# Latent attention with a ring of six PSUM banks, and its values multiplied token by token with a column of ones

## The chip, the cores and the metric

The kernel runs on one NeuronCore of a Trainium2 chip. A NeuronCore has a TensorE (matrix multiply; PE in the profile, and PEld for its loads of the stationary operand), a VectorE (DVE), a ScalarE (ACT), a GpSimd (POOL) and DMA queues, which run side by side and meet through semaphores. Matmul results go into PSUM, eight banks of 128 partitions by 512 float32. The metric is the device time of one execution in microseconds, and the median of several runs is compared.

## What is computed

Four layers follow one another on 8 sequences of 256 tokens of width 128: a minGRU, six blocks of local attention with a feed-forward, a latent attention with grouped heads, and a mixture of eight experts. The change touches the third one. The printed reference leaves the body of this layer to the reader, so it is given here as the kernel computes it (16 query heads, 4 key heads, head width 8, causal, scale 8^-0.5):

```
cq  = norm(x) @ Wqa ; q = rope(cq @ Wqb)            # 16 heads of 8
ckv = norm(x) @ Wkva; k, v = ckv @ Wkvb             # 4 heads of 8 each, k with rope
S   = q k^T + causal                                # per head 256 x 256
p   = exp(S - rowmax(S))
o   = (p @ v) / sum(p)
x   = x + o @ Wout + bout
```

Four query heads share one key head. The quotient o has 16 x 8 = 128 columns for each token.

## The kernel before

The latent stage is written out in Python for steps s = 1 to 11 (`pairs`). At step s the engines work on several sequences at once: s is being normalised and projected, a = s - 1 has its attention, c = s - 2 is finished (quotient, output projection, gate moments), and s - 3 and s - 4 choose their experts. `live(k)` says whether sequence s - k exists. Each engine has its own instruction stream (`lat_pe`, `lat_act`, `lat_dve`, `lat_pool`), in a fixed order written by hand. Nothing is reordered at run time.

A sequence's attention is cut into three parts, called quads here: m = 0 (first 128 tokens, four query heads for each key head, 128 keys), m = 1 and m = 2 (last 128 tokens, two query heads each, 256 keys). A quad has four groups r = 0 to 3, one for each key head. In a quad TensorE does this, in order:

- `scores`: four matmuls into banks 4 to 7 (L1429), and four that add the causal mask (L1435). They wait until all four `exp` of the quad before are done.
- small work of other sequences: normalisation transposes, projections, the gate's logits and counts (L1350, L1356, L1357, L1343, L1493, L1505, L1522, L1528, L1535).
- `values` of the quad before: L1465, see below.
- `turns`: the four tiles of p are transposed, four 128x128 transposes for each r (L1450), into bank 2 (r = 0, 2) and bank 3 (r = 1, 3). So r = 2 waits until ScalarE has copied r = 0 out of bank 2 (L1564), and r = 3 until VectorE has copied r = 1 out of bank 3 (L1651).

VectorE takes the row maxima (L1613) and ScalarE the exponentials (L1575) between scores and turns.

`values` before: the stationary operand is 32 columns wide, `cvj`, which holds v in 8 of the 32 columns and zeros in the others, and the moving operand is 128 columns of turned p. Four r go side by side into four groups of 32 columns of the array, and the result lies turned, features by tokens, in bank 1. A second set of matmuls with `conesb` (ones in place of v) makes the sums of p, one copy for each feature. In bank 1, columns 0 to 255 hold the numerators and 256 to 511 the denominators. VectorE then takes 128x256 reciprocals (L1624) and multiplies (L1626) into `con`, which is already the stationary operand of the output projection (L1522). GpSimd spreads v into `cvj` once a sequence (L1680), from `cvn`, which ScalarE copied out of PSUM (L1591).

After the latent stage the experts' stage sorts tokens and multiplies them; its code is not touched.

Of the kernel before, what the change touches and what calls it, by code (L numbers as in the profile page):

```python
# [13 lines left out]
ALU = mybir.AluOpType  # L14
# [4 lines left out]
P = 128  # L19
# [77 lines left out]
def mixed_kernel(nc, A, out):  # L97
    with ExitStack() as ctx:  # L98
# [80 lines left out]
        cvn = sb("cvn", [P, NT, KVH, QD])  # L179
        conesb = sb("conesb", [P, GRP, 32])  # L180
# [8 lines left out]
        cvj = sq[:, :, :].rearrange("p h d -> p (h d)").rearrange("p (k r j x) -> p k r j x", k=NT, r=KVH, j=GRP)  # L189
        late = attT[:, :, :].rearrange("p c k -> p (c k)")  # L190
        con, crd = late[:, 0:SEQ], late[:, SEQ:2 * SEQ]
# [6 lines left out]
        for a, b in ((t1, t2), (None, None), (pr, ob), (pr, ob)):  # L198
# [115 lines left out]
        c_mq, c_mk, c_cq, c_ck, cv_ev, c_cv = (sig(x, credit=2) for x in ("c_mq", "c_mk", "c_cq", "c_ck", "cv_ev", "c_cv"))  # L314
# [3 lines left out]
        c_vz, c_one = sig("c_vz"), sig("c_one")  # L318
# [29 lines left out]
            "pool": (tabs, ln_ve, ln_rs, sq_half, q_add, k_add, q_norm, k_norm, c_cq, c_ck, c_cv),  # L348
# [107 lines left out]
        NG = NQ * KVH  # L456

# [888 lines left out]
        def choose_logits(pe, g):  # L1346
            pe.wait_ge(g_out.sem, g_out.after(g))
            pe.wait_ge(d_ch.sem, d_ch.after(g - 1, PLACE))
            for t in range(NT):
                mm = pe.matmul(bank[3][:, t * NE:(t + 1) * NE], xnG[:, t * P:(t + 1) * P], wg[:, :], start=True, stop=True)  # L1350
            mm.then_inc(d_lmm.sem, 1)
# [12 lines left out]
        def choose_bias(dve, g):  # L1364
            dve.wait_ge(d_lmm.sem, d_lmm.after(g))
            link(dve, dve.tensor_tensor(dlg[:, :, :], bank[3][:, 0:NT * NE].rearrange("p (t e) -> p t e", t=NT),
                                        bgb[:, :].unsqueeze(1).broadcast_to([P, NT, NE]), ALU.add), g, LOGIT)
# [48 lines left out]
        def lat_pe(pe):  # L1416
            low, high = bank[0][:, 0:SEQ], bank[0][:, SEQ:2 * SEQ]

            def scores(a, ap, m):
                t, j0, nh, nk = QUADS[m]  # L1420
                G = NG * a + KVH * m
                if m == 0:
                    pe.wait_ge(c_cq.sem, c_cq.after(a))
                    pe.wait_ge(c_ckm.sem, c_ckm.after(a, 1))
                if m == 1:
                    pe.wait_ge(c_ckm.sem, c_ckm.after(a))
                pe.wait_ge(c_exp.sem, c_exp.after(G - 1))
                for r in range(KVH):
                    pe.matmul(bank[4 + r][:, :], cq[32 * r:32 * r + 32, ap * SEQ + t * P:ap * SEQ + (t + 1) * P],  # L1429
                              ckm[32 * r:32 * r + 32, ap * GRP + j0:ap * GRP + j0 + nh, 0:nk * P], start=True, stop=False,  # L1430
                              skip_group_check=True)
                for r in range(KVH):
                    tri = causal[:, t, :].rearrange("p (h b k) -> p h b k", h=nh, b=nk)[:, :, nk - 1, :]
                    diag = bank[4 + r][:, :].rearrange("p (h b k) -> p h b k", h=nh, b=nk)[:, :, nk - 1, :]
                    pe.matmul(diag, identb[:, :], tri, start=False, stop=True, skip_group_check=True).then_inc(c_s.sem, 1)  # L1435

            def turns(a, m, g):
                for r in range(KVH):
# [8 lines left out]
                    ev, n = (c_pta, c_ptd)[r % 2], 2 * (NQ * a + m) + r // 2  # L1447
                    pe.wait_ge(ev.sem, ev.after(n - 1))
                    for q in range(4):
                        mm = pe.transpose(bank[2 + r % 2][:, q * P:(q + 1) * P], cp[:, r, q * P:(q + 1) * P], ident)  # L1450
                    mm.then_inc(c_pt.sem, 1)

            def values(a, m):
                t, j0, nh, nk = QUADS[m]
                n = NQ * a + m
                pe.wait_ge(c_pta.sem, c_pta.after(2 * n + 1))
                pe.wait_ge(c_ptd.sem, c_ptd.after(2 * n + 1))
                if m == 0:
                    pe.wait_ge(c_cv.sem, c_cv.after(a))
                    pe.wait_ge(c_nrm.sem, c_nrm.after(a - 1))  # L1460
                for x in range(4):
                    j, kb = j0 + x // nk, x % nk
                    for o, ones in ((0, False), (SEQ, True)):
                        for r in range(KVH):
                            mm = pe.matmul(bank[1][32 * r:32 * r + 32, o + t * P:o + (t + 1) * P],  # L1465
                                           conesb[:, j, :] if ones else cvj[:, kb, r, j, :], cpT[r][:, x * P:(x + 1) * P],
                                           start=(m == 0 and x == 0 and not ones), stop=(x == 3), skip_group_check=True)
# [4 lines left out]
            pe.wait_ge(c_one.sem, 2)  # L1472
            pe.wait_ge(ld_late.sem, 16 * (BLANKS + 1))
            for s, par, live in pairs():
                a, c = s - 1, s - 2
                for m in range(NQ):
                    if live(1):
                        scores(a, 1 - par, m)
                    if m == 0 and live(4):
                        n = NQ * c + 2 if live(2) else NQ * NB - 1  # L1480
                        pe.wait_ge(c_ptd.sem, c_ptd.after(2 * n + 1))
                        choose_counts(pe, s - 4)
                    if m == 1 and live(3):
                        n = NQ * a if live(1) else NQ * NB - 1
                        pe.wait_ge(c_ptd.sem, c_ptd.after(2 * n + 1))
                        choose_logits(pe, s - 3)
                    if m == 0:
# [7 lines left out]
                        if live(3):  # L1495
                            n = NQ * c + 2 if live(2) else NQ * NB - 1
                            pe.wait_ge(c_pta.sem, c_pta.after(2 * n + 1))
# [9 lines left out]
                    if m == 1:  # L1507
# [6 lines left out]
                        if live(2):  # L1514
                            pe.wait_ge(c_nrm.sem, c_nrm.after(c))
# [4 lines left out]
                            for t in range(NT):  # L1520
                                y = low[:, t * P:(t + 1) * P]
                                mm = pe.matmul(y, con[:, t * P:(t + 1) * P], wout[:, :], start=True, stop=True)  # L1522
# [23 lines left out]
        def lat_act(act):  # L1546
            act.preload_act_table(ACT.Exp)
            for s, par, live in pairs():
                a = s - 1
                for m in range(NQ):  # L1550
# [11 lines left out]
                    def keep_turned(r):  # L1562
                        act.wait_ge(c_pt.sem, c_pt.after(NG * a + KVH * m + r))
                        act.activation(cpT[r], bank[2][:, :], ACT.Copy).then_inc(c_pta.sem, 1)  # L1564

                    for r in range(KVH):
                        if live(1):
                            G = NG * a + KVH * m + r
                            if m == 0 and r == KVH - 1:
                                keep_turned(0)  # L1570
# [3 lines left out]
                            for hh in range(nh):  # L1574
                                ins = act.activation(cp[:, r, hh * n:(hh + 1) * n], bank[4 + r][:, hh * n:(hh + 1) * n],  # L1575
# [11 lines left out]
                    if live(1):  # L1587
                        if m == 0:
                            act.wait_ge(c_pv.sem, c_pv.after(a))
                            act.wait_ge(c_cv.sem, c_cv.after(a - 1))  # L1590
                            act.activation(cvn[:, :, :, :].rearrange("p t r d -> p (t r d)"),  # L1591
                                           bank[0][:, SEQ:SEQ + NT * KVH * QD], ACT.Copy).then_inc(cv_ev.sem, 1)
                        if m:
                            keep_turned(0)
                        keep_turned(2)

        def lat_dve(dve):
# [3 lines left out]
            dve.wait_ge(ld_late.sem, 16 * (BLANKS + 1))  # L1601
            dve.tensor_scalar(run, cst("region"), ident[:, 0:1], None, ALU.mult)
            for s, par, live in pairs():
                a, c = s - 1, s - 2
                for m in range(NQ):
# [3 lines left out]
                    if live(1):  # L1609
                        for r in range(KVH):  # L1610
                            G = NG * a + KVH * m + r
                            dve.wait_ge(c_s.sem, c_s.after(G))
                            dve.tensor_reduce(cnb[:, r, 0:nh], bank[4 + r][:, :].rearrange("p (h k) -> p h k", h=nh), AX.X,  # L1613
# [5 lines left out]
                    if m == 0:  # L1619
                        if live(0):  # L1620
                            ln_moments(dve, LN_C + s, tokens(s))
                        if live(2):
                            dve.wait_ge(c_o.sem, c_o.after(NQ * c + 2))
                            dve.reciprocal(crd, bank[1][:, SEQ:2 * SEQ]).then_inc(c_nrm.sem, 1)  # L1624
                            dve.wait_ge(c_nrm.sem, c_nrm.after(c, 1))
                            dve.tensor_tensor(con, bank[1][:, 0:SEQ], crd, ALU.mult).then_inc(c_nrm.sem, 1)  # L1626
# [8 lines left out]
                    if m == 1 and live(2):  # L1635
                        dve.wait_ge(c_y.sem, c_y.after(c))
                        dve.tensor_tensor(acc[:, seq_cols(c)], bank[0][:, 0:SEQ], acc[:, seq_cols(c)], ALU.add).then_inc(c_res.sem, 1)
# [10 lines left out]
                    if live(1):  # L1648
                        for r in (1, 3):
                            dve.wait_ge(c_pt.sem, c_pt.after(NG * a + KVH * m + r))  # L1650
                            dve.tensor_copy(cpT[r], bank[3][:, :]).then_inc(c_ptd.sem, 1)  # L1651
                            if m == 0 and r == 1 and live(-1):
                                add_stream(dve, s + 1)
                    elif m == 0 and live(-1):
# [6 lines left out]
        def lat_pool(pool):  # L1661
# [4 lines left out]
            pool.memset(conesb[:, :, :], 0.0).then_inc(c_one.sem, 1)  # L1666
            pool.wait_ge(c_one.sem, 1)
            for j in range(GRP):
                ins = pool.memset(conesb[:, j, j * QD:(j + 1) * QD], 1.0)
            ins.then_inc(c_one.sem, 1)  # L1670
            pool.wait_ge(add_u.sem, 1)
            pool.wait_ge(ld_late.sem, 16 * (BLANKS + 1))
            pool.memset(cvj, 0.0).then_inc(c_vz.sem, 1)
            pool.wait_ge(c_vz.sem, 1)

            def values(s):
                pool.wait_ge(cv_ev.sem, cv_ev.after(s))
                hold(pool)
                for j in range(GRP):
                    ins = pool.tensor_copy(cvj[:, :, :, j, j * QD:(j + 1) * QD], cvn[:, :, :, :])  # L1680
                ins.then_inc(c_cv.sem, 1)

            for s, par, live in pairs():
                if live(0):
                    ln_rsqrt(pool, LN_C + s)
                if live(1):
                    pool.wait_ge(ln_stats.sem, ln_stats.after(ln_seq(s - 1)))
                    x = tokens(s - 1)
                    pool.tensor_tensor(x, x, boutb[:, :].unsqueeze(1).broadcast_to([P, NT, D]), ALU.add)
                    values(s - 1)  # L1690
# [328 lines left out]
```

## Time and profile before

| | |
|---|---|
| median of 3 runs | 2133.55 us (2131.57 to 2133.88) |
| profiled execution | 2131.08 us, span of the trace 2129.2 us |
| TensorE, VectorE, ScalarE, GpSimd busy | 1999.3, 1534.3, 1692.5, 1455.5 us |
| first and last scores of the latent stage begin | 1792.7 and 1992.3 us |
| its last values end | about 2002.7 us |

The trace gives for each instruction its engine, source line, operands, start and length. Idle time of an engine is put down to the instruction that released it. PEclk is the granted clock of TensorE: 1.00 is 2.4 GHz, 0.50 is 1.2 GHz. An f32 matmul leaves two records, each with a weight load of its own; a transpose leaves one. A matmul's record is longer than the time until the next one may start, since they are pipelined, so what a block costs is read from starts.

### The profile page before, as it was taken

To read this page: it belongs to the slowest core of one execution; us is meant where nothing else is said; L and a number is where in the kernel's file an instruction comes from. 1 tells how busy PE (TensorE), PEld (TensorE's weight loads), DVE (VectorE), ACT (ScalarE), POOL (GpSimd) and SP (SyncE) were. 2 spreads that over 40 slices of the span, in tenths; PEclk is the share of its full clock that TensorE was granted. 3 is DMA by queue.
4 is the path that set the end of the run, shared out by engine and by line. 5 is a ranking of instruction groups with operands and counts; after the bars stand their busy time and mean duration, and the time that the engine had idled before them with its cause. 6 is when DMAs were issued, how large, how long until landed. Compare 5 with 4: busy or idle time off the path is not lost. (4 is left out here: it accounts for less than half of the span.)

```text
span 2129.2 us, 64823 instructions
## 1 busy us (share of the span) xinstructions
PE 1999.3 (94%) x21611; PEld 1399.3 (66%) x21611; DVE 1534.3 (72%) x3516; ACT 1692.5 (79%) x4279; POOL 1455.5 (68%) x1662
## 2 busy tenths in 40 slices
PE   6799999999999999999999999999999997988696
PEld 3466666666666666666666666666666665655486
DVE  5777777777777777777777777777777764788654
ACT  3589898989898989898989898989898985655355
POOL 4687878787878787878787878777777762244343
PEclk8899999999999999999999999999999999999888
DMA  3232223222233222323222322223544242000023
GB/s 96 49 72 55 57 71 82 64 57 54 59 84 75 56 58 53 90 63 68 52 59 69 84 62 59 52 60 83 119 98 103 51 105 84 2 12 11 15 61 107
DMA packets 191396, 138.95 MB, mean 65 GB/s; under 512 B 47758, under 2 KB 183636, under 8 KB 191172
## 3 DMA queue, kind: packets, MB, share of 16 engines
q1 hardware_dynamic: 189028, 133.09, 26.4%
q0 software_dynamic: 2272, 4.72, 0.7%
q8 instruction: 42, 0.69, 0.1%
q14 instruction: 54, 0.44, 0.1%
HBM read 28.36 MB, written 14.96 MB: 20 GB/s over the span
## 5 line engine op out<-in xcount | busy, mean ns | idle before, releaser
L975 ACT ACTIVATE pr<-bank,mx 128x64 f32<-128x64 f32 x1536 | 336.9, 348 | 0.3 <-DVE mx L1078 0.2
L1160 POOL TENSOR_TENSOR qr<-t 128x512 f32<-128x512 f32 x192 | 245.8, 1280 | 130.4 <-DVE t L1058 130.3
L1057 DVE TENSOR_TENSOR t<-bank,rot_t 128x512 f32<-128x512 f32 x384 | 262.8, 684 | 99.7 <-PE bank L813 93.5
L1148 POOL TENSOR_TENSOR qr<-qr,rn 128x512 f32<-128x512 f32 x192 | 201.0, 1047 | 173.3 <-DVE rn L1029 173.3
L1058 DVE TENSOR_TENSOR t<-bank,rot_t 128x512 f32<-128x512 f32 x384 | 261.1, 680 | 0.0
L1163 POOL TENSOR_TENSOR kr<-t 128x512 f32<-128x512 f32 x192 | 245.7, 1280 | 1.0 <-DVE t L1058 1.0
L1166 POOL TENSOR_TENSOR sqh<-sq 128x512 f32<-128x512 f32 x192 | 245.6, 1279 | 0.0
L937 ACT ACTIVATE sq<-bank 128x512 f32<-128x512 f32 x192 | 114.3, 596 | 156.1 <-DVE t L1058 151.6
L983 ACT ACTIVATE kBD<-bank 64x512 f32<-64x512 f32 x384 | 229.0, 596 | 3.1 <-PE bank L530 0.8
L813 PE MATMUL bank<-wqkv,xs 128*128 128x512 f32 x384 | 208.1, 624 | 9.3 <-issue 6.4
L864 PE MATMUL bank<-kBD,qT 128*32 128x128 f32 x6144 | 207.5, 276 | 0.4 <-ACT bank L918 0.3
L878 PE MATMUL bank<-vBD,pT 128*32 128x128 f32 x6144 | 206.4, 275 | 0.2 <-ACT pT L941 0.2
L1089 DVE TENSOR_TENSOR ob<-bank,rinv 128x512 f32<-128x512 f32 x192 | 132.1, 688 | 98.4 <-PE bank L878 98.3
L1148 POOL TENSOR_TENSOR kr<-kr,rn 128x512 f32<-128x512 f32 x192 | 201.0, 1047 | 0.0
L836 PE MATMUL bank<-wqkv,xs 128*128 128x512 f32 x384 | 200.8, 605 | 0.0
L817 PE MATMUL bank<-wqkv,xs 128*128 128x512 f32 x384 | 198.7, 599 | 0.0
L864 PEld LDWEIGHTS bank<-kBD,qT 128*32 128x32 f32 x6144 | 156.1, 109 | 61.1 <-issue 60.2
L897 PE MATMUL bank<-attT,wo 128*128 128x256 f32 x768 | 186.4, 385 | 0.0
L1099 DVE TENSOR_REDUCE ss<-sqh 128x16 f32<-128x512 f32 x192 | 130.7, 681 | 75.8 <-POOL sqh L1166 70.1
L878 PEld LDWEIGHTS bank<-vBD,pT 128*32 128x32 f32 x6144 | 159.9, 110 | 33.6 <-issue 33.1
L1078 DVE TENSOR_REDUCE mx<-bank 128x8 f32<-128x512 f32 x192 | 131.8, 687 | 65.5 <-PE bank L864 65.5
L897 PEld LDWEIGHTS bank<-attT,wo 128*128 128x128 f32 x768 | 141.5, 189 | 27.3 <-ACT vS L956 8.7
(252 smaller groups left out, 4332.6 us busy)
## 6 DMA issues: line engine op xcount, KB each, us to landing
vBD<-vS SPq DMA_DIRECT2D x1152, 64.0 KB, 2.0
vBD<-vS SPq DMA_DIRECT2D x576, 32.0 KB, 1.8
wqkv<-in_L_ffn_Wqkv_dram SPq DMA_DIRECT2D x12, 768.0 KB, 6.6
rows<-const SPq DMA_DIRECT2D x4, 2244.0 KB, 11.2
wo<-in_L_ffn_Wo_dram SPq DMA_DIRECT2D x12, 256.0 KB, 2.9
t<-rows SPq DMA_DIRECT2D x39, 66.0 KB, 1.8
vBD<-in_L_ffn_W_dram SPq DMA_DIRECT2D x1, 2048.0 KB, 8.5
vBD<-in_L_ffn_W_dram SPq DMA_DIRECT2D x8, 256.0 KB, 7.1
```

What stands on the lines that cost most here:

```text
L813: pe.matmul(bank[0][:, :], xt, wqkv[:, h * 512:(h + 1) * 512], start=True, stop=True).then_inc(q_mm.sem, 1)
L864: mm = pe.matmul(bank[5][w * WIN:(w + 1) * WIN, p * P:(p + 1) * P], qT[:, slot % 2, p, w * WIN:(w + 1) * WIN], kBD[:, h, p, :, k0:k0 + 2 * ...
L878: mm = pe.matmul(bank[7][w * WIN:(w + 1) * WIN, p * P:(p + 1) * P], pT[:, p, w * WIN:(w + 1) * WIN], vBD[:, h, t * NWT + w, :, p, :], star ...
L897: mm = pe.matmul(bank[2][:, 0:SEQ], wo[:, h * HP + c, :], attT[:, h * HP + c, :], start=(c == 0), stop=(c == HP - 1))
L975: ins = act.activation(pr[:, slot % 2, hd, :], bank[5][:, hd * 64:(hd + 1) * 64], ACT.Exp, bias=mx[:, slot % 2, hd:hd + 1])
L983: ins = act.activation(kBD[64 * e:64 * e + 64, h, :, e, WIN + t * P:WIN + (t + 1) * P], bank[4][64 * e:64 * e + 64, :].rearrange("p (a b) ...
L1057: dve.tensor_tensor(t1[:, m], src, tab[:, 0, :].unsqueeze(1).broadcast_to([P, HH, DH]), ALU.mult)
L1058: dve.tensor_tensor(t2[:, m].rearrange("p h (s d) -> p h s d", s=2), swp, tab[:, 1, :].rearrange("p (s d) -> p s d", s=2).unsqueeze(1).bro ...
L1148: pool.tensor_tensor(x, x, rn[:, slot, half * HH:(half + 1) * HH].unsqueeze(2).broadcast_to([P, HH, DH]), ALU.mult).then_inc(norm.sem, 1)
L1160: pool.tensor_tensor(qr[:, slot].rearrange("p (h d) -> p h d", d=DH), t1[:, 0], t2[:, 0], ALU.add).then_inc(q_add.sem, 1)
L1163: pool.tensor_tensor(kr[:, slot], t1[:, 1], t2[:, 1], ALU.add).then_inc(k_add.sem, 1)
L1166: pool.tensor_tensor(sqh[:, :, :], sq[:, :, 0:DH // 2], sq[:, :, DH // 2:], ALU.add).then_inc(sq_half.sem, 1)
```

## The change

- The turned p and the scores share six banks in a ring, `RING = (4, 5, 6, 7, 2, 3)`. The scores of a quad take four of them, the turned tiles r = 0, 1 the two others, and r = 2, 3 the first two score banks, whose exponentials are done. No transpose waits for a copy of its own quad any more. It waits for the copies r + 2 of the quad before, and the scores r = 2, 3 wait for the copies r - 2 of the quad before.
- The copies out of PSUM are split anew: ScalarE takes (0, 2), (0, 1, 2), (0, 2) and VectorE the rest, where each took two. ScalarE's copy r = 0 of m = 0 no longer stands between two exponentials.
- `values`: turned p is now the stationary operand, 128x128, and the moving one is v with a column of ones, 9 columns (`cvo`). The result lies tokens by (head, 9), with the sum of p in the ninth column. There are 16 matmuls for each quad where there were 32. `cvj`, `conesb` and GpSimd's spreading go; ScalarE copies v straight into `cvo`.
- The reciprocal is of 128x32 elements, and the product is tokens by features. So it has to be turned for its projection: two transposes on TensorE into bank 1 (L1560 of the changed kernel), behind the turns of m = 0, and a 128x256 copy on ScalarE at the head of m = 1 (L1588). `values(a, 0)` and the projection wait for that copy (`c_keep`).
- The gate's logits move from bank 3 to bank 5, and GpSimd's addition of the bias raises `c_bias`, for which VectorE's residual waits.

```diff
+        RING = (4, 5, 6, 7, 2, 3)
+        COPY_ACT = ((0, 2), (0, 1, 2), (0, 2))
+        COPY_DVE = tuple(tuple(r for r in range(KVH) if r not in x) for x in COPY_ACT)
+        def score_bank(m, r):
+            return bank[RING[(2 * m + r) % len(RING)]]
+        def turn_bank(m, r):
+            return bank[RING[(2 * m + KVH + r) % len(RING)]] if r < 2 else score_bank(m, r - 2)
...
                 for r in range(KVH):
-                    pe.matmul(bank[4 + r][:, :], cq[...
+                    if r >= 2 and n:
+                        wait_turned(pe, *divmod(n - 1, NQ), r - 2)
+                    pe.matmul(score_bank(m, r)[:, :], cq[...
...
-                    ev, n = (c_pta, c_ptd)[r % 2], 2 * (NQ * a + m) + r // 2
-                    pe.wait_ge(ev.sem, ev.after(n - 1))
+                    n = NQ * a + m
+                    if r < 2 and n:
+                        wait_turned(pe, *divmod(n - 1, NQ), r + 2)
...
-                    for o, ones in ((0, False), (SEQ, True)):
-                        for r in range(KVH):
-                            mm = pe.matmul(bank[1][32 * r:32 * r + 32, o + t * P:o + (t + 1) * P],
-                                           conesb[:, j, :] if ones else cvj[:, kb, r, j, :], cpT[r][:, x * P:(x + 1) * P],
+                    for r in range(KVH):
+                        mm = pe.matmul(outs[:, t, r * GRP + j, :], cpT[r][:, x * P:(x + 1) * P], cvo[:, kb, r, :],
...
+                    if m == 0 and live(2):
+                        pe.wait_ge(c_nrm.sem, c_nrm.after(c))
+                        for t in range(NT):
+                            mm = pe.transpose(bank[1][:, t * P:(t + 1) * P], con[:, t].rearrange("p h d -> p (h d)"), ident)
+                        mm.then_inc(c_turn.sem, 1)
...
+                    if m == 1 and live(2):
+                        act.wait_ge(c_turn.sem, c_turn.after(s - 2))
+                        act.activation(conT, bank[1][:, 0:SEQ], ACT.Copy).then_inc(c_keep.sem, 1)
...
+                        if live(1):
+                            keep_turned(a, 0, 1)
                         if live(2):
                             dve.wait_ge(c_o.sem, c_o.after(NQ * c + 2))
-                            dve.reciprocal(crd, bank[1][:, SEQ:2 * SEQ]).then_inc(c_nrm.sem, 1)
+                            dve.reciprocal(crd, outs[:, :, :, QD]).then_inc(c_nrm.sem, 1)
```

How the change stands in TensorE's stream, at the end of the values and the turns of m = 0 in a step with all sequences live (s = 5). Before, from the last eight of the 32 value matmuls to the next scores:

```order
L1465 MATMUL bank1<-vS,sq 32x128 x4
L1465 MATMUL bank1<-vS,conesb 32x128 x4
L1505 MATMUL bank0<-wvb,ckva 128x32 x2
L1450 MATMUL bank2<-const,qr 128x128 x4
L1450 MATMUL bank3<-const,qr 128x128 x4
L1450 MATMUL bank2<-const,qr 128x128 x4
L1450 MATMUL bank3<-const,qr 128x128 x4
L1429 MATMUL bank4<-kBD 128x512
```

The same place in the changed kernel, all 16 value matmuls in one row:

```order
L1363 MATMUL bank2<-const,t1 128x128 x2
L1487 MATMUL bank1<-sq,vS 128x9 x16
L1523 MATMUL bank0<-wvb,ckva 128x32 x2
L1473 MATMUL bank2<-const,qr 128x128 x4
L1473 MATMUL bank3<-const,qr 128x128 x4
L1473 MATMUL bank4<-const,qr 128x128 x4
L1473 MATMUL bank5<-const,qr 128x128 x4
L1560 MATMUL bank1<-const,attT 128x128 x2
L1451 MATMUL bank6<-kBD 128x512
```

The four transposed tiles now have four banks, and two transposes of the quotient stand between them and the next scores.

VectorE at the same place, from the last maximum of m = 0 on, before:

```order
L1613 TENSOR_REDUCE cnb<-bank7 128x4
L394 BN_STATS lnst<-acc 128x6 x2
L400 BN_AGGR lnmv<-lnst 128x2 x2
L1624 RECIPROCAL attT<-bank1 128x256
L1626 TENSOR_TENSOR attT<-bank1,attT 128x256
L1651 COPY vS<-bank3 128x512
L1034 TENSOR_TENSOR xT<-xT,uT 128x256
L1651 COPY vS<-bank3 128x512
```

and in the changed kernel:

```order
L1638 TENSOR_REDUCE cnb<-bank7 128x4
L395 BN_STATS lnst<-acc 128x6 x2
L401 BN_AGGR lnmv<-lnst 128x2 x2
L1625 COPY vS<-bank3 128x512
L1651 RECIPROCAL attT<-bank1 128x32
L1653 TENSOR_TENSOR attT<-bank1,attT 128x256
L1625 COPY vS<-bank5 128x512
L1054 TENSOR_TENSOR xT<-xT,uT 128x256
```

The copy of r = 1 has moved ahead of the reciprocal, which is now 32 elements wide.

## Rows read from the trace of the kernel before

**Rows 1.** Stretches: length, busy PE, PEld, DVE, ACT, POOL, PEclk, DMA share, GB/s.

```profile
1792.00:1993.00 201.00, 174.10 (x2289) 119.63 (x2288) 155.47 (x382) 116.16 (x341) 69.59 (x124) 1.00 0.03 8
```

**Rows 2.** PE by line, 1792.7 to 2003: busy, mean ns, idle before, releasers.

```profile
L1450 PE MATMUL bank<-const,qr 128*128 128x128 f32 x384 | 55.2, 279 | 26.2 <-ACT vS L1564 14.8 <-DVE vS L1651 10.8 <-ACT qr L1575 0.6
```

**Rows 3.** Timeline of PE, quad m = 0: start, length, line, idle before.

```profile
1894.56 1.14 PE L1429 MATMUL bank<-kBD 32*128 32x512 f32 x8
...
1897.44 0.42 PE L1465 MATMUL bank<-vS,sq 128*32 128x128 f32 x8
...
1897.90 0.40 PE L1465 MATMUL bank<-vS,sq 128*32 128x128 f32 x8
...
1899.32 0.63 PE L1505 MATMUL bank<-wvb,ckva 32*128 32x32 f32 x4
1899.88 1.10 PE L1450 MATMUL bank<-const,qr 128*128 128x128 f32 x8
1901.94 0.63 PE L1450 MATMUL bank<-const,qr 128*128 128x128 f32 x4 [0.96 <-ACT vS L1564]
1903.03 0.63 PE L1450 MATMUL bank<-const,qr 128*128 128x128 f32 x4 [0.47 <-DVE vS L1651]
1903.59 0.71 PE L1429 MATMUL bank<-kBD 32*128 32x512 f32 x4
```

**Rows 4.** Timeline of PE, turns of a quad m = 2 and the next scores.

```profile
1891.29 1.09 PE L1450 MATMUL bank<-const,qr 128*128 128x128 f32 x8
1892.72 0.63 PE L1450 MATMUL bank<-const,qr 128*128 128x128 f32 x4 [0.34 <-ACT vS L1564]
1894.00 0.63 PE L1450 MATMUL bank<-const,qr 128*128 128x128 f32 x4 [0.65 <-DVE vS L1651]
```

**Rows 5.** The gate's logits: loads by line (ns min/median/max), and one timeline row.

```profile
L1350 PEld LDWEIGHTS bank<-wg,uT x32: 186/192/338, 1851.5 to 2016.5; 128*128 128x128 f32 x32
2002.73 0.52 PEld L1350 LDWEIGHTS bank<-wg,uT 128*128 128x128 f32 x4 [0.20 <-issue]
```

**Rows 6.** Scores on PE by line: duration ns, first and last start.

```profile
L1429 PE MATMUL bank<-kBD x192: 587/625/692, 1792.7 to 1992.7; 32*128 32x512 f32 x192
```

**Rows 7.** Timeline of DVE in the quad of rows 3, and a small reciprocal.

```profile
1900.10 1.72 DVE L1624 RECIPROCAL attT<-bank 128x256 f32<-128x256 f32 x1
1901.86 0.42 DVE L1626 TENSOR_TENSOR attT<-bank,attT 128x256 f32<-128x256 f32 x1
1902.20 0.68 DVE L1651 COPY vS<-bank 128x512 f32<-128x512 f32 x1
1750.61 0.20 DVE L1067 RECIPROCAL rinv<-psm 128x8 f32<-128x8 f32 x1
```

**Rows 8.** Timeline of ACT in the quad of rows 3.

```profile
1901.09 0.71 ACT L1564 ACTIVATE vS<-bank 128x512 f32<-128x512 f32 x1
1901.57 1.26 ACT L1575 ACTIVATE qr<-bank,cnb 128x128 f32<-128x128 f32 x4
```

**Rows 9.** Timeline at the stage's end: the last projection on PE.

```profile
2005.21 0.71 PE L1522 MATMUL bank<-wout,attT 128*128 128x128 f32 x4 [1.86 <-DVE attT L1626]
```

**Rows 10.** Stretches as in rows 1, and PE by line for two of them.

```profile
1779.50:1789.60 10.10, 8.35 (x19) 5.04 (x18) 2.35 (x4) 3.85 (x7) 6.87 (x15) 0.50 1.14 332
1796.50:1799.90 3.40, 2.22 (x16) 1.67 (x16) 1.86 (x7) 3.40 (x15) 1.61 (x3) 1.00 0.01 2
2028.70:2032.00 3.30, 3.30 (x30) 3.08 (x29) 2.74 (x8) 2.23 (x3) 1.14 (x2) 1.00 0.12 41
2032.10:2038.80 6.70, 4.52 (x21) 3.96 (x20) 4.49 (x14) 0.57 (x3) 0.00 (x0) 0.50 0.23 51
L1714 PE MATMUL bank<-b2e,vS 8*128 8x128 f32 x32 | 4.4, 299 | 0.0
```

**Rows 11.** Timeline of PE: the same twelve matmuls at either clock.

```profile
1766.51 2.96 PE L503 MATMUL bank<-xnF,w 128*128 128x256 f32 x12
1783.93 5.46 PE L503 MATMUL bank<-xnF,w 128*128 128x256 f32 x12 [0.75 <-issue]
```

More of the change, by code:

```diff
@@ L456, in mixed_kernel, with turned, wait_turned @@
         NG = NQ * KVH
+        RING = (4, 5, 6, 7, 2, 3)
[5 more added lines that the diff above has]
+            return bank[RING[(2 * m + KVH + r) % len(RING)]] if r < 2 else score_bank(m, r - 2)
+        def turned(a, m, r):
+            x, who = (c_pta, COPY_ACT) if r in COPY_ACT[m] else (c_ptd, COPY_DVE)
+            return x, sum(map(len, who)) * a + sum(map(len, who[:m])) + who[m].index(r)
+        def wait_turned(eng, a, m, r):
+            x, n = turned(a, m, r)
+            eng.wait_ge(x.sem, x.after(n))
         LAG = 3
@@ L1349, in choose_logits @@
             for t in range(NT):
-                mm = pe.matmul(bank[3][:, t * NE:(t + 1) * NE], xnG[:, t * P:(t + 1) * P], wg[:, :], start=True, stop=True)
+                mm = pe.matmul(bank[5][:, t * NE:(t + 1) * NE], xnG[:, t * P:(t + 1) * P], wg[:, :], start=True, stop=True)
             mm.then_inc(d_lmm.sem, 1)
@@ L1495, in lat_pe @@
                         if live(3):
-                            n = NQ * c + 2 if live(2) else NQ * NB - 1
-                            pe.wait_ge(c_pta.sem, c_pta.after(2 * n + 1))
+                            wait_turned(pe, c if live(2) else NB - 1, 2, 2)
                             choose_turn(pe, s - 3, 1 - par)
@@ L1589, in lat_act @@
                             act.wait_ge(c_pv.sem, c_pv.after(a))
[L1590 to L1595, printed above, removed]
+                            act.activation(cvo[:, :, :, 0:QD], bank[0][:, SEQ:SEQ + NT * KVH * QD].rearrange("p (t r d) -> p t r d", t=NT, r=KVH),
+                                           ACT.Copy).then_inc(cv_ev.sem, 1)
+                        for r in COPY_ACT[m]:
+                            act.wait_ge(c_pt.sem, c_pt.after(NG * a + KVH * m + r))
+                            act.activation(cpT[r], turn_bank(m, r)[:, :], ACT.Copy).then_inc(c_pta.sem, 1)
         def lat_dve(dve):
@@ L1636, in lat_dve @@
                         dve.wait_ge(c_y.sem, c_y.after(c))
+                        dve.wait_ge(c_bias.sem, c_bias.after(c))
                         dve.tensor_tensor(acc[:, seq_cols(c)], bank[0][:, 0:SEQ], acc[:, seq_cols(c)], ALU.add).then_inc(c_res.sem, 1)
@@ L1648, in lat_dve @@
                     if live(1):
[L1649 to L1654, printed above, removed]
+                        for r in COPY_DVE[m][1 if m == 0 else 0:]:
+                            keep_turned(a, m, r)
+                    if m == 0 and live(-1):
                         add_stream(dve, s + 1)
@@ L1665, in lat_pool @@
             pool.tensor_copy(identb[:, :], ident).then_inc(cast_done.sem, 1)
[L1666 to L1671, printed above, removed]
-            pool.wait_ge(ld_late.sem, 16 * (BLANKS + 1))
[L1673 to L1681, printed above, removed]
+            pool.memset(cvo[:, :, :, :], 1.0).then_inc(c_one.sem, 1)
+            pool.wait_ge(ld_late.sem, 16 * (BLANKS + 1))
             for s, par, live in pairs():
```

68 lines of the change are left out of this document (33 added, 35 removed).

## The prediction

> **What bounds the kernel now.** I read the stretches first, since the change touches one stage of four. In the 201 us from the first to the last scores of the latent stage [rows 1, 6] the reader is to see that TensorE has 174 us of busy time, VectorE 155, ScalarE 116, GpSimd 70, that DMA does next to nothing (share 0.03), and that TensorE's clock is 1.00. Then the lines of TensorE [rows 2]: of its idle time in the stage, 26.2 us stand in front of the transposes of p, 14.8 waiting for ScalarE's copy out of bank 2 and 10.8 for VectorE's out of bank 3. Only 0.6 us wait for an exponential. Then one quad in order of time [rows 3]: from scores at 1894.56 to scores at 1903.59 there is no hole of TensorE but the two in front of the third and fourth group of transposes, 0.96 and 0.47 us. So TensorE's own stream, with these holes in it, is the length of the stage. A quad of a full step lasts 9.03 us, and there are 24 of them. What the change does to the time is what it does to TensorE's stream, plus any new hole.
>
> **The values.** Before, eight records begin every 0.22 or 0.23 us (1897.44, then sixteen records later 1897.90) [rows 3]: four matmuls of 32 stationary columns run side by side. A quad has 32 matmuls, 64 records, so 1.76 us (1897.44 to 1899.32 with the change-over to the next line). After, a quad has 16 matmuls, 32 records, each with its own load of 128x128 f32 and only 9 columns to stream. The trace has this shape almost exactly: the logits, 128x128 stationary and 8 columns moving. Four loads take 0.52 us, one alone 0.19 [rows 5], so they begin (0.52 - 0.19) / 3 = 0.11 us apart. The nine columns themselves hide under the next load. 32 x 0.11 = 3.52 us. The block gets 3.52 - 1.76 = 1.76 us longer, and 24 of them give **+42.2 us**. Halving the matmuls doubles the time, because the four that ran side by side now run one after another, and the 128 columns that were streamed are now loaded.
>
> **The ring.** Both holes go. The transposes r = 0 to 3 go to four banks whose last readers were the copies and exponentials of earlier work. **-26.2 us** [rows 2]. Each hole also cost the change-over behind it: the turns of a quad m = 2 last from 1891.29 to the scores at 1894.56, 3.27 us, of which 0.34 and 0.65 are holes, so 2.28 net [rows 3, 4]. Eight transposes in a row take 1.09 us, of which the last record is about 0.28, so 0.12 each and 0.47 for a group. Four groups and a change-over are 2.0 us. 0.28 less, 24 times, is -6.7; I take **-6.5**. Will the exponentials now be late? In the longest case, rows 3, the last one ends at 1902.83, 8.3 us after the scores began, with a copy of 0.71 us put between [rows 8]. Without that copy it comes some 0.5 us sooner, 7.8 us. After the change the values (3.52) push the first group to about 2.88 + 3.52 + 0.56 = 7.0 us and the fourth to 8.4. So no exponential is waited for: TensorE has become later than they are. In the first quad of all there are no values to push it, and there the exponentials decide: of its idle time I expect a third back at most, which is **+1** against the terms above.
>
> **The quotient.** The 128x256 reciprocal of 1.72 us becomes one of 32 elements, near the 0.20 us of 128x8; the product stays 0.42 [rows 7]. That time is VectorE's. But a new link is in TensorE's stream: two transposes behind the turns of m = 0, 0.25 us for each of 8 sequences, **+2.0**, and they wait for VectorE. In VectorE's order the copy of r = 1 now stands ahead of the reciprocal, though the values that it needs ended long before. Counted from the scores: the second group of transposes begins at 7.45 us and its record is 0.63 long, copy from 8.1 to 8.75 (0.68), reciprocal and its semaphore 0.4, product 0.42, semaphore 0.1: 9.65 us. TensorE is free at 7.0 + 4 x 0.47 = 8.9. A hole of some 0.7 us, in the 7 steps in which scores follow: **+5**. Behind it on TensorE are the scores of m = 1, on which VectorE and ScalarE wait. ScalarE's copy of the turned quotient (0.4 us, by its like of 256 columns) lies at the head of m = 1, where ScalarE waits for the first maximum anyway; TensorE asks for it two microseconds later. If that cover were gone it would cost 0.4 us, 8 times.
>
> **The end.** The last projection waited 1.86 us for the product [rows 9]. Reciprocal, product, two transposes and a copy with their semaphores are about 2.1 us where reciprocal and product were 2.5: **-0.5**.
>
> **At nothing:** GpSimd's spreading of v and its memsets (GpSimd is busy a third of the stage, and v is wanted two microseconds after it is spread); `c_bias` (GpSimd adds it in the quad before); the logits' bank; the new split of copies. ScalarE's three copies in m = 1 end about 2.6 us after the turns begin, the scores that need the second of them come after 3.1 us of TensorE's work.
>
> **Sum:** 42.2 - 26.2 - 6.5 + 1 + 2.0 + 5 - 0.5 = +17.0, with 0.5 for the wait ahead of the last values (a copy that now comes alone) **+17.5 us**. The profiled execution took 2131.1 us, of which the span is 2129.2; it lies 2.5 under the median of the runs, within their spread. On the median: 2133.5 + 17.5 = **2151 us**. Bounds of this case: if a record costs 0.10 us and the new hole is nothing, 2151 - 8 - 5 = 2138; if the holes come out at twice 0.7 and the turns save nothing, 2151 + 5 + 6.5 = 2163.
>
> **Rivals.** *The clock falls.* After the change TensorE spends 3.5 us at a time in which it streams 9 columns for each load of 128. Rows of this kernel show falls behind narrow work of a busy TensorE. Between 2028.7 and 2032.0 TensorE is busy all the time, with loads and matmuls of 8 of 128 rows (L1714), at 1.00 (2.4 GHz), and directly behind it the clock is 0.50 (1.2 GHz) for 6.7 us; between 1779.5 and 1789.6 it is 0.50 at a busy share of 0.83; between 1796.5 and 1799.9 it stays 1.00 at 0.65, with full-array transposes [rows 10]. A value block after the change is busy and narrow like the first of these, in its streaming if not in its loads. At the lower clock the same twelve matmuls take 5.46 us where they took 2.96 [rows 11], so a spell of low clock gives back half its length. If each of the 24 blocks brings a spell of about 5 us (the trace has 6.7 and 10.1, and dense scores and turns follow), 24 x 2.5 = +60: 2211 us. With 6.7 us, +80: 2231. Against it: the rows before the fall had loads of 8 rows, those of the value block are full ones, and no row shows a long run of these with little streaming. The Trainium skill ("TensorE: Matmul & The Clock Gate", section on how the gate's oscillation bites in real kernels) gives as its abstract rule that there be no long idle gaps of TensorE. By that rule the clock would stay, as the new stream has fewer gaps, and the sum would be 2151; the fall behind 2028.7 to 2032.0, with no gap, is against it, and the measurement decides.
>
> *The loads hide (the other side).* If the 9 columns set the pace and not the load, the block shrinks instead. The change breaks even at 3.52 - 17.5 / 24 = 2.8 us for a block, 0.087 us for a record. At 0.03 a block is about 1 us, and the sum is -18 - 26.2 - 6.5 + 8 = -43, of which the exponentials' chain, 8 us in m = 0, leaves about -30: 2103 us. For it speaks only that the matmul itself is short. Against it the 0.11 of rows 5, measured on this shape. The same skill's page, section on packing small matmuls, puts three column tiles at 2.38 times one; giving up four is against this rival too.
>
> *TensorE is not the bound*, and the 1.76 us fall into holes that something else keeps: no change, 2133. Against it: three quads of 9.03 us are 27.1, less their holes (3 x 26.2 / 24 = 3.3) and plus 3 x 1.76 = 5.3 they are 29.1 us of TensorE's own work, over what a step takes now.
>
> *A copy is late*: six banks are all in use, and the scores r = 2, 3 need copies of the quad just turned. If ScalarE is 0.5 us late in each quad, +12: 2163.
>
> **Chances.** Forecast 0.49, clock 0.36, late copy 0.06, loads hidden 0.05, no bound 0.04. The range goes from 2140 to 2225, which leaves out the other side, the lowest edge of my own case and the longer spells. Within 0.2% (4 us, about what a measurement can tell here): 0.04; faster 0.05, slower 0.91. The likeliest case's own range is 2138 to 2163.
>
> **What would show it.** The value matmuls as 32 records with starts 0.11 us apart, 3.5 us a quad; no idle time in front of the transposes of p; two transposes of the quotient with an idle of about 0.7 us released by VectorE's product; quads of 9.4 to 10 us in full steps where they were near 9.0; granted clock 1.00 through the stage. Wrong if PEclk in the stage is under 0.9 (then the second case), if records begin under 0.09 us apart, or if the time in front of the transposes stays.

## The result and the profile after

The changed kernel takes 2197.4 us (median of 4 runs, 2190.8 to 2203.1) where the kernel before takes 2132.9 (4 runs, 2131.6 to 2133.9): 1.030 times as long, interval 1.026 to 1.033. It is 64.5 us slower. The sign was forecast, and the time lies in the range of 2140 to 2225, but the likeliest case (2151) did not happen. What happened is the rival "the clock falls", priced at 2211.

The profiled execution took 2192.5 us with a span of 2190.7, against 2131.1 and 2129.2 before. The page of the changed kernel, busy times and TensorE's granted clock in 40 slices of some 55 us:

```profile
PE 2086.2 (95%) x20859; PEld 1494.3 (68%) x20859; DVE 1519.6 (69%) x3508; ACT 1700.7 (78%) x4295; POOL 1446.3 (66%) x1625
...
PEclk8899999999999999999999999999999988778788
```

Over the whole execution TensorE has 87 us more of busy time, with 752 records fewer. The latent stage is slices 33 to 38, and the clock there is 0.7 to 0.8. The same from stretches: the whole stage (first scores to last values), then six stretches of two quads in order, and three of the spells in which the clock is low. The columns are those of [rows 1].

```profile
1789.90:2064.20 274.30, 270.83 (x1688) 221.27 (x1688) 147.42 (x396) 130.47 (x368) 66.29 (x98) 0.79 0.02 6
1914.30:1917.00 2.70, 2.70 (x17) 1.28 (x16) 1.62 (x6) 1.18 (x4) 0.91 (x2) 1.00 0.00 0
1917.10:1920.20 3.10, 3.10 (x28) 3.10 (x28) 3.00 (x11) 2.59 (x8) 1.23 (x2) 0.95 0.00 0
1920.60:1927.40 6.80, 6.80 (x29) 5.44 (x32) 2.34 (x6) 1.20 (x2) 1.99 (x4) 0.55 0.00 0
1927.60:1930.90 3.30, 3.30 (x28) 2.59 (x25) 3.04 (x9) 1.05 (x5) 0.40 (x1) 1.00 0.00 0
1930.90:1934.20 3.30, 3.30 (x28) 3.22 (x28) 1.11 (x5) 3.30 (x15) 1.41 (x3) 0.90 0.02 5
1934.30:1937.30 3.00, 3.00 (x16) 2.81 (x14) 1.36 (x3) 1.57 (x5) 0.09 (x1) 0.55 0.00 0
...
1919.90:1926.70 6.80, 6.80 (x28) 5.83 (x27) 2.58 (x7) 1.12 (x2) 2.69 (x4) 0.50 0.00 0
1933.50:1936.90 3.40, 3.40 (x18) 3.34 (x18) 0.96 (x2) 1.97 (x8) 0.89 (x2) 0.51 0.00 0
1943.80:1947.20 3.40, 3.40 (x19) 3.40 (x17) 0.61 (x3) 1.60 (x3) 2.41 (x3) 0.50 0.10 32
```

The reader is to see two things. TensorE is busy for 270.8 of 274.3 us, where it was busy for 87% of the stage before [rows 1], and all the same its mean clock is 0.79. And the spells at 0.50 (1.2 GHz) go with the value blocks. All 24 blocks begin at 1.00; in 22 of them or right behind them the clock falls, and it is back at 1.00 near the end of the transposes (from 0.7 us before it to 2.2 us behind it; the last spell runs on beyond the stage). Only two short spells of 3.4 us, from 1790.2 and 1797.0, lie ahead of the first value block (1801.3) and don't come from one. Next the timeline of TensorE over the same two quads.

```profile
1914.34 1.14 PE L1451 MATMUL bank<-kBD 32*128 32x512 f32 x8
...
1917.01 4.38 PE L1487 MATMUL bank<-sq,vS 128*128 128x9 f32 x32
1921.32 2.07 PE L1553 MATMUL bank<-cqa,wqb 64*128 64x256 f32 x4
1923.32 3.61 PE L1473 MATMUL bank<-const,qr 128*128 128x128 f32 x16
1926.86 1.14 PE L1451 MATMUL bank<-kBD 32*128 32x512 f32 x8
...
1929.64 3.64 PE L1487 MATMUL bank<-sq,vS 128*128 128x9 f32 x32
...
1933.90 3.45 PE L1473 MATMUL bank<-const,qr 128*128 128x128 f32 x16
1937.38 0.44 PE L1560 MATMUL bank<-const,attT 128*128 128x128 f32 x2
1937.75 0.71 PE L1451 MATMUL bank<-kBD 32*128 32x512 f32 x4
```

The structure is the forecast one. The second value block, at full clock, takes 3.6 us. No hole stands in front of the transposes of p or behind them. But the sixteen transposes take 3.5 us where 2.0 were expected, because they run at 0.50, and a quad is 12.5 us (1914.34 to 1926.86) or 10.9 (1926.86 to 1937.75) where 9.4 to 10 were forecast.

The lines of TensorE in the stage: busy, mean ns, idle before, which answer to [rows 2].

```profile
L1487 PE MATMUL bank<-sq,vS 128*128 128x9 f32 x768 | 97.7, 268 | 0.0
L1473 PE MATMUL bank<-const,qr 128*128 128x128 f32 x384 | 78.0, 387 | 0.6 <-ACT qr L1596 0.6
...
L1560 PE MATMUL bank<-const,attT 128*128 128x128 f32 x14 | 3.3, 321 | 1.4 <-DVE attT L1653 1.2
```

The 26.2 us of idle time in front of the transposes are gone (0.6 left). They were converted, not saved: the same 384 transposes have a mean record of 387 ns where it was 279 [rows 2], and from their first records to the next line's they take 79.4 us in all where they took 80.6.

**Where the 61.4 us of the profiled executions are.** The stage is 274.4 us long where it was 210.1. Added up over its records of the clock, 117.1 us of it are at 0.50 (6.8 ahead of the first value block, 110.3 from there on). Half of that, 58.5 us, is time lost if TensorE was at work throughout. It began 2.8 us earlier, since the spell of low clock that lies ahead of the stage [rows 10, 11] fell a little differently, and behind the stage both kernels take 126 us. 64.3 - 2.8 = 61.5, which is the 61.4 but for rounding. Without the 58.5 the stage would be 215.9 us, which is 5.8 above before and not 17.5; but that is no price of the terms, since at the low clock TensorE is late and waits of some microseconds are covered by it. The experiments have to separate the two.

### The profile page after: what moved, and what is told of

Read it like the earlier page. It is cut to its first block and busy times, and to the rows that moved or that the text cites. A ratio compares the mean times of both kernels' runs of the same rounds, so it can differ in the third digit from the quotient of the medians.

```text
span 2190.7 us, 63247 instructions
## 1 busy us (share of the span) xinstructions
PE 2086.2 (95%) x20859; PEld 1494.3 (68%) x20859; DVE 1519.6 (69%) x3508; ACT 1700.7 (78%) x4295; POOL 1446.3 (66%) x1625
## 5 line engine op out<-in xcount | busy, mean ns | idle before, releaser
L1077 DVE TENSOR_TENSOR t<-bank,rot_t 128x512 f32<-128x512 f32 x384 | 263.0, 685 | 99.0 <-PE bank L833 92.7
```

Of the source, the lines that this page charges most:

```text
L1077: dve.tensor_tensor(t1[:, m], src, tab[:, 0, :].unsqueeze(1).broadcast_to([P, HH, DH]), ALU.mult)
```

## Experiments

Every time is a median; the kernel before ran on the same chip beside each (2130.5 to 2131.6 us).

### Does the streaming hold the clock? 36, 72 and 144 columns

The two theories: the clock falls because so few columns are streamed for each load (theory A), or because of the run of full loads, the new order or the lost gaps, whatever is streamed (theory B). The value matmuls keep their loads, their number, their order and their waits. Only the moving operand is widened: v and its ones stand between zeros, and a window of 4, 8 or 16 heads is streamed, so that the other heads get zeros added. The zeros are multiplied and added in vain; nothing is left out. With `WG` = 4, 8 and 16 there are 36, 72 and 144 columns.

```diff
-        cvo = sq[:, :, :].rearrange("p h d -> p (h d)")[:, 0:NT * KVH * (QD + 1)].rearrange("p (k r d) -> p k r d", k=NT, r=KVH)
+        WG = 8
+        WC, WPAD = (QD + 1) * WG, (QD + 1) * (WG - 1)
+        cvz = sb("cvz", [P, NT, KVH, 2 * WPAD + QD + 1])
+        cvo = cvz[:, :, :, WPAD:WPAD + QD + 1]
...
-                        mm = pe.matmul(outs[:, t, r * GRP + j, :], cpT[r][:, x * P:(x + 1) * P], cvo[:, kb, r, :],
+                        h = r * GRP + j
+                        w0 = WPAD - (QD + 1) * (h % WG)
+                        o = (t * QH + h // WG * WG) * (QD + 1)
+                        mm = pe.matmul(bank[1][:, o:o + WC], cpT[r][:, x * P:(x + 1) * P], cvz[:, kb, r, w0:w0 + WC],
```

Expected of 72 columns:

> The changed kernel, with the moving operand of each value matmul widened from 9 to 72 columns by zeros on both sides of v and its ones (eight heads' window, accumulated in place); 32 records and loads a quad as before, same result. Clock theory (the slowdown is mostly TensorE's clock, which falls behind blocks that stream 9 columns a load): 72 columns take 0.06 us and hide under the load of 0.11, so the blocks stay 3.5 us at full clock, the granted clock of the stage is 1.00 throughout, and the time is 2192 less half of the 115 us at 0.50, so 2135 to 2145 us. Rival (the serial loads and new waits make the slowdown, the clock is incidental or goes by something else): low clock stays, 2190 us or more.

Expected of 36 columns:

> As the run with 72 columns, but a window of 36. Clock theory: streaming is 0.03 of 0.11 us, still narrow; some falls of the clock remain, less than with 9 columns: 20 to 100 us of the stage at 0.50, 2145 to 2185 us. Rival (any widening helps, or none does): equal to the run with 72, or equal to the changed kernel at 2197.

Expected of 144 columns:

> As the run with 72 columns, but a window of 144 (all sixteen heads). Streaming takes 0.12 us a record and sets the pace in place of the load: a block is 3.84 us, 0.3 more than with 72, 24 times: 7 to 8 us over the run with 72. Clock 1.00 in both. Rival: loads and streaming of one record add up instead of overlapping; then a block is over 7 us and the time over 2200.

Measured: 72 columns 2143.8 us (2141.8 to 2147.0, 4 runs), ratio 1.0057 (1.0039 to 1.0076); 36 columns 2184.7 and 144 columns 2153.8, one run each. The whole stage as a stretch, with 36, then 72, then 144 columns:

```profile
1793.30:2056.30 263.00, 258.40 (x1680) 212.45 (x1688) 147.60 (x396) 130.10 (x368) 66.37 (x98) 0.82 0.02 6
```

```profile
1792.90:2018.90 226.00, 218.08 (x1680) 175.08 (x1688) 147.07 (x396) 128.44 (x368) 66.48 (x98) 0.98 0.02 7
...
1804.00:2018.90 214.90, 208.56 (x1637) 170.19 (x1642) 141.15 (x381) 122.83 (x348) 64.87 (x95) 1.00 0.03 8
```

```profile
1792.80:2026.20 233.40, 224.66 (x1680) 182.21 (x1688) 147.00 (x396) 128.96 (x368) 66.36 (x98) 1.00 0.02 7
```

| columns streamed | stage, us | at 0.50, us | start to start of a load, us |
|---|---|---|---|
| 9 (changed kernel) | 274.4 | 117.1 (6.8 before 1801.3) | 0.112 |
| 36 | 263.0 | 92.7 | 0.112 |
| 72 | 226.0 | 6.8 (before 1804) | 0.112 |
| 144 | 233.4 | 0 | 0.122 |

The same number of instructions with eight times the columns is 54 us faster, because the clock stays at 1.00 from 1804 on. Theory B falls: loads, order and waits are the same in all four (the padded operand has a buffer of its own and is filled by a second memset, but so it is with 36 columns, and there the clock falls). Theory A holds for these blocks, and the cost of the clock is measured: 2197.4 - 2143.8 = 53.6 us. 36 columns came out at the upper edge of what was expected, in one run.

The 6.8 us that 72 columns have left are the same two short spells ahead of the first value block (here 1804.2) that the changed kernel has. With 144 columns they are not there, and the two kernels show what they cost, from the first scores to the first values with 72, then with 144 columns:

```profile
1792.90:1804.20 11.30, 9.72 (x47) 5.09 (x49) 6.12 (x16) 5.61 (x20) 1.60 (x3) 0.70 0.01 2
```

```profile
1792.80:1802.20 9.40, 7.00 (x47) 3.95 (x49) 6.19 (x16) 5.59 (x20) 1.60 (x3) 1.00 0.01 3
```

That is 2.0 us (1.96 by the first records) and not half of 6.8, because TensorE isn't busy throughout there. The 72 columns are free, since the load sets the pace (0.112 us as with 9). At 144 the columns set it: a value block takes 4.02 us where it took 3.62, 9.7 us over the 24. That is nearly the whole of the 9.4 us by which this stage is longer than 226.0 less the 2.0 (between the medians 10.0, where 7 to 8 were expected). The kernel with 72 columns also shows what the terms of the prediction are at full clock; one quad m = 0 with 72 columns, to be read beside [rows 3]:

```profile
1903.88 1.14 PE L1454 MATMUL bank<-kBD 32*128 32x512 f32 x8
...
1906.67 3.69 PE L1493 MATMUL bank<-cvz,vS 128*128 128x72 f32 x32
1910.29 0.63 PE L1529 MATMUL bank<-wvb,ckva 32*128 32x32 f32 x4
1910.85 1.97 PE L1476 MATMUL bank<-const,qr 128*128 128x128 f32 x16
1913.45 0.44 PE L1566 MATMUL bank<-const,attT 128*128 128x128 f32 x2 [0.64 <-DVE attT L1659]
1913.82 0.71 PE L1454 MATMUL bank<-kBD 32*128 32x512 f32 x4
```

Here the quad is as it was drawn in the prediction: 9.94 us (the two others of a step take 9.12 and 9.35), values 3.6, the turns in one piece 1.97, and a hole of 0.64 us in front of the quotient's transposes, released by VectorE's product.

The Trainium skill ("TensorE: Matmul & The Clock Gate", section on why this matters for your kernels) advises for matmuls with a thin M to do all of K before the next DMA or to pad M, with the reason that otherwise the clock oscillates. Padding helped here too, but it was the moving operand that was padded; no run here pads M. The section on the oscillation, which the prediction quoted, lays it to idle gaps of TensorE. Here the changed kernel's stage, with 3.5 us of gaps, is at 0.79, and that of the kernel before, with 26.9 [rows 1], at 1.00; the measurement decides.

### The ring alone

The kernel before with the ring of six banks, the new split of copies and the moved copy r = 1, but with its own values, reciprocal and quotient.

```diff
+        RING = (4, 5, 6, 7, 2, 3)
+        COPY_ACT = ((0, 2), (0, 1, 2), (0, 2))
...
-                    pe.wait_ge(ev.sem, ev.after(n - 1))
+                    if r < 2 and n:
+                        wait_turned(pe, *divmod(n - 1, NQ), r + 2)
...
                         if live(2):
                             dve.wait_ge(c_o.sem, c_o.after(NQ * c + 2))
                             dve.reciprocal(crd, bank[1][:, SEQ:2 * SEQ]).then_inc(c_nrm.sem, 1)
```

> The kernel before with the ring of six banks, the new split of copies and VectorE's early copy, but the old values (32 stationary columns side by side, 128x256 reciprocal, no turn of the quotient). Theory: the holes of 26.2 us in front of the transposes go, and 6.5 us of change-overs: 2100 us. Rival: without them the exponentials or the copies are late, and half of it comes back as waits: 2115 us. Other side: nothing gained, 2133.

Measured: 2115.4 us (2114.5 to 2117.2), ratio 0.9928 (0.9912 to 0.9945), 16 us faster. The stage, and what TensorE waits for in it (total us, times, longest):

```profile
1790.80:1987.40 196.60, 178.60 (x2435) 126.57 (x2443) 156.55 (x396) 123.66 (x361) 72.54 (x130) 1.00 0.03 9
```

```profile
PE bank L1470 <- ACT qr L1585: 5.3, 14, 0.4
PE bank L1448 <- POOL kBD L1144: 4.1, 5, 0.9
PE bank L1559 <- DVE acc L1654: 2.4, 4, 0.6
PE bank L387 <- issue: 2.2, 5, 1.1
```

No transpose and no scores wait for a copy any more (the gate's counts do once, 0.8 us), so the mechanism is right, but alone it gives half of the 32.7 us that the sum has for it, as the rival in the expectation had it. TensorE now arrives early: it waits for exponentials (L1585), for the key matrix that GpSimd prepares (L1144) and for VectorE's sum (L1654). From the first transpose of a quad to the next line's first record, summed over the 24 quads, it is 63.0 us where it was 80.6. The prediction said so for one place ("TensorE has become later than they are"). That no exponential is waited for holds beside the longer values, not beside the old ones.

### The ring alone, with the copy where it stood

As the last kernel, but VectorE's copy r = 1 of m = 0 stands behind reciprocal and product again.

```diff
-                        if live(1):
-                            keep_turned(a, 0, 1)
                         if live(2):
...
-                        for r in COPY_DVE[m][1 if m == 0 else 0:]:
+                        for r in COPY_DVE[m]:
```

> The kernel with the ring alone (2115 us), but VectorE's copy of r = 1 back behind reciprocal and product in m = 0. The reciprocal is 1.72 us wide there, so theory: copy r = 1 comes 2 us later and the fourth scores of m = 1 wait for it, 3 to 8 us slower than the ring alone. Rival: the product was what the next projection waited for, and it gets 3 to 8 us faster.

Measured: 2113.4 us (2110.4 to 2116.4), ratio 0.9918 (0.9899 to 0.9936). The stage of the profiled execution is 192.2 us, 4.4 shorter than in the last one. The theory that this is slower by 3 to 8 us falls; whether it is faster than the ring with the moved copy the medians, 2 us apart with overlapping runs, don't say. It has the lowest median of all kernels tried, 17 us under the kernel before and 84 under the changed one.

### The values alone, with 9 columns

The changed kernel with its transposes back in banks 2 and 3 (r = 2, 3 wait for the copies of their own quad), and ScalarE's copy r = 0 between the exponentials.

```diff
-            return bank[RING[(2 * m + r) % len(RING)]]
+            return bank[4 + r]
...
-            return bank[RING[(2 * m + KVH + r) % len(RING)]] if r < 2 else score_bank(m, r - 2)
+            return bank[2 + r % 2]
...
+                    if r >= 2:
+                        wait_turned(pe, a, m, r - 2)
```

> The changed kernel without the ring: scores in banks 4 to 7, turned tiles in banks 2 and 3, two copies on each engine, as before the change; the new values (128x128 stationary, 9 columns streamed) and the turn of the quotient stay. Clock theory with my terms: 2132 + 42 (values) + 2 + 5 (turn of the quotient and its hole), holes of the transposes kept, and 55 to 60 for the clock: 2235 us, granted clock of the stage near 0.8. Rival (ring and values share one gain, as the longer values hide the holes): under 2210 us.

Measured: 2214.4 us (2204.0 to 2223.0), ratio 1.0384 (1.0342 to 1.0426). The stage and its transposes:

```profile
1792.10:2085.40 293.30, 288.16 (x1680) 227.66 (x1688) 153.20 (x404) 125.77 (x360) 66.28 (x98) 0.74 0.02 6
```

```profile
L1472 PE MATMUL bank<-const,qr 128*128 128x128 f32 x384 | 85.9, 397 | 1.6 <-ACT vS L1593 1.3 <-ACT vS L1617 0.3
```

The stage is at 0.50 for 153.7 us, more than with the ring (117.1), and of the 26.2 us of waits for copies 1.6 are left. So the holes that the ring removes hardly exist here: the longer values and the low clock had hidden them already. The clock falls with or without the ring, so the new values are its cause. Why the low share is larger without the ring is not settled; the time came out between the two expectations.

### The values alone, with 72 columns

The last kernel with the padded window of the first experiment.

> The new values with a window of 72 columns, so at full clock, but without the ring: banks 2 and 3 for the turned tiles, two copies on each engine. Against the run with 72 columns and the ring (2144 us) it shows what the ring is worth to the new values when the clock is out of the way. Theory of my sum: the holes of 26 us and 6.5 us of change-overs come back: 2144 + 33 = 2177 us. Rival: beside a longer value block the ring is worth what it was worth to the kernel before, 15 to 17 us (there measured as 2132 against 2115): 2160 us.

Measured: 2161.2 us (2160.5 to 2163.6), ratio 1.0141 (1.0122 to 1.0161); 7.6 us of the stage at 0.50. TensorE's waits:

```profile
PE bank L1475 <- ACT vS L1623: 5.5, 16, 0.3
PE bank L1475 <- ACT vS L1599: 3.3, 8, 1.0
PE bank L1475 <- ACT qr L1604: 2.2, 7, 0.3
```

At full clock the copies are waited for again, but the holes sum up to 8.8 us and not 26.2, so the rival in the expectation (2160) holds. The new values alone cost 29.8 us, where the sum without the ring's terms says 50; the ring beside them is worth 2161.2 - 2143.8 = 17.4 us, nearly the 16 that it is worth beside the old ones. 29.8 - 17.4 = 12.4 is the change at full clock. Both differences shrank against the prediction, and what is left of them differs from its +17.5 by only 5. The transposes show why. From their first records to the next line's they take 80.6 us before, 63.0 with the ring alone, 65.0 with the 72-column values alone and 52.5 with both. The longer block alone fills about half of the holes without any ring, so a hole is counted once, in whichever of the two is taken first.

### The hole in front of the quotient's transposes

The kernel with 72 columns and the ring, with VectorE's copy r = 1 put back behind the product, by the same edit as above.

> The run with 72 columns (2144 us), but VectorE's copy of r = 1 behind the product, which needs only values that ended long before. Theory: TensorE's hole of 0.8 us in front of the quotient's transposes (12.6 us in 16 waits) goes in the 7 steps in which scores follow: 5 to 6 us faster, 2138. Rival: the scores of m = 1 then wait for the later copy: same time.

Measured: 2140.2 us (2140.0 to 2141.3, 5 runs), ratio 1.0042 (1.0027 to 1.0056). What the loads of the quotient's transposes waited for in the whole execution (total us, times), with the copy ahead of the reciprocal and then behind the product:

```profile
  DVE attT L1659: 12.6, 16
```

```profile
  DVE attT L1657: 2.1, 2
```

The quads m = 0 of full steps go from 9.93 to 9.08 us, and the stage from 226.0 to 220.3, 5.8 for the 5 that the prediction has for this hole. The medians, of two chips, differ by 3.7, and the intervals of the two ratios overlap, so it is the trace that carries this: by it, the moved copy costs what it was said to.

## Why the prediction was half right

**The step that failed** is the choice of the likeliest case: that the clock stays at 1.00 through the stage (0.49) against that it falls (0.36). "No row shows a long run of these with little streaming" was true, and it was weighed as if it spoke for the clock. The row that bore on it, a TensorE busy all the time with narrow work ahead of a fall [rows 10], was set aside because its loads have 8 rows and those of the value block are full. The runs showed that full loads don't hold the clock: with 9 streamed columns the stage is at 0.50 for 117.1 us, with 72 and the same loads for 6.8. The size of the rival was good: 24 spells of 5 us, 120 us, for 22 spells of 5.0 us on average, 110.3 us, and +60 for 53.6 between the medians. The measured time lies in the range only because the range was drawn to take in this rival; by the likeliest case, 2138 to 2163, it is 34 us off at the nearest.

**The terms** of the sum, at full clock, are measured in the kernels with 72 columns. The +1, -0.5 and +0.5 for the first quad and the end are not measured apart. The first four rows add up TensorE's starts from the first record of a block to the first of the next line:

| term | forecast | measured |
|---|---|---|
| value blocks | +42.2 | 3.62 for 1.88 with the change-over, 1.74 x 24 = +41.8 |
| holes and change-overs of the transposes | -26.2 - 6.5 | 80.6 to 46.9 over 24 quads (the copy put back), -33.7 |
| quotient's transposes | +2.0 | 8 x 0.37 = +3.0 |
| their hole | +5 | 52.5 - 46.9 = +5.6 |
| all, between medians | +17.5 | +12.3 (ratio 1.0039 to 1.0076, so 8 to 16) |

The loads begin 0.112 us apart for a forecast of 0.11, so "the loads hide" and "TensorE is not the bound" are refuted: 24 blocks did get longer, and the stage with them. The four terms are each within 1 us and give 16.7. In two quads of three, scores to values are also 0.09 us shorter (2.88 us in [rows 3], 2.79 in the quad above), -1.5 in all, which the prediction doesn't have. That makes 15.2. The stage got 13.9 longer (15.9, less the 2.0 that the two short spells cost). Of the 1.3 between them, 0.5 is the low clock in the first quad's transposes (3.59 us, and 3.12 with 144 columns) and 0.4 the eighth pair of the quotient's transposes, which comes behind the last values; the other 0.4 are the matmuls of the output projection, which take 3.45 us up to the next line's where they took 3.84. One reading of the prediction is loose without touching the sum: 9.03 us is the first quad of a full step, and the 23 quads up to the last scores take 8.7 on average.

**Late copies** did not come: neither scores nor transposes wait for a copy in the changed kernel's stage. **The moved copy** costs its 5 us only at full clock; in the changed kernel itself TensorE waited 1.2 us there in the stage, because VectorE kept its speed and TensorE had become slow. **The ring's worth** of 32.7 us is the second step that was wrong, and the sum hides it. The -33.7 in the table is what ring and longer values do together. The ring by itself is worth 16 us beside the old values and 17 beside the new ones; the rest of the holes went because the longer value block filled them. That the term fits within 1 us is no proof of the reasoning behind it.

## What to carry to other kernels

When a matmul's wide operand is made the stationary one, its columns move from the stream into the loads: look at the streamed columns and at the granted clock, and not only at busy time, because here a stage 99% busy ran at half clock for 43% of its length. If the load sets the pace, widen the moving operand up to the length of the load: here 72 columns for 9, with zeros, cost nothing and gave back 54 of 64 us. (Real columns in place of the zeros were not run.) And try each half of a change alone: the half that freed banks was 16 us faster by itself, the half that reordered the values was slower in all seven forms that were run, by 0.4 to 3.8%.

## What the runs showed of the hardware

Zeros served to hold the clock: seven in eight of the 72 streamed columns are zeros, and the stage is at 1.00 from 1804 on. The effect is graded: from the first value block on, 110, 93, 0 and 0 us at 0.50 for 9, 36, 72 and 144 columns behind the same loads (36 and 144 in one run each). A full f32 load is the pace of a record up to 72 columns at least (0.112 us from start to start), and at 144 it is 0.122. And a low clock is not a loss of its own size: from its first value block on the changed kernel has 110.3 us at 0.50, half of which is 55.2, but the padded kernel, with none there, is 48.4 us shorter over the same stretch. Of the 6.8 between them 3.2 are a wait that the slow TensorE had covered and that comes back (4.4 us for 1.2 in front of the quotient's transposes). The rest is not told apart.
